# An attention and adapter block on one core: P V as eight 64x32 tiles, score bursts of two pairs on six banks

## What is computed

```python
h = _layernorm(x) * (1 + ca) + sa
qkv = (h @ qkv_w.T).reshape(B, S, 3, 16, 16)          # 16 heads of width 16
scores = jnp.einsum('bhqd,bhkd->bhqk', q, k) * scale
probs = jax.nn.softmax(scores, axis=-1)
out = jnp.einsum('bhqk,bhkd->bhqd', probs, v)
x = x + ga * (out @ proj_w.T + proj_b)
h = _layernorm(x) * (1 + cb) + sb
# 8 encoders and decoders are tried on h, the one with the least loss is chosen, and its
# adapter (W_down, W_up) is added to h @ W_base + b_base
x = x + gb * ffn(h)
```

## Time and profile before

| | before |
|---|---|
| median of 3 runs | 971.86 us |
| the profiled execution's own time | 975.65 us |
| its span in the trace | 973.8 us |
| busy: PE matmul | 938.1 us, 96% |
| busy: PE weight load | 489.1 us, 50% |
| busy: VectorE | 792.8 us, 81% |
| busy: ScalarE | 656.7 us, 67% |
| busy: GpSimd | 373.6 us, 38% |
| chain that ended last | PE 76%, DVE 10%, ACT 4%, DMA 3% |

### The profile page before, as it was taken

How to read it: one execution, slowest core, us unless ns; L and a number is a source line. 1 busy time by engine, 2 the same in 40 slices (tenths; PEclk the granted TensorE clock), 3 DMA queues, 4 the chain that set the end, 5 groups by cost and what they waited for, 6 DMA issues and landing times.

```text
span 973.8 us, 16714 instructions
## 1 busy us (share of the span) xinstructions
PE 938.1 (96%) x5890; PEld 489.1 (50%) x5890; DVE 792.8 (81%) x1629; ACT 656.7 (67%) x1295; POOL 373.6 (38%) x497
## 2 busy tenths in 40 slices
PE   6899999999999999999999999999999899999997
PEld 4443344434444555555444555645445465644486
DVE  4799989999788888877897888876887778888365
ACT  2148888888588677666679677575777756667930
POOL 4050265225366354121746645121655312115320
PEclk9889999999899999999999999999999999999999
DMA  7832061253444210555150511526123500141101
GB/s 179 142 73 45 23 115 58 60 122 82 70 75 77 59 45 25 83 82 168 48 86 20 94 57 35 83 54 170 52 64 53 77 8 29 41 129 59 30 6 50
DMA packets 51427, 68.78 MB, mean 71 GB/s; under 512 B 12347, under 2 KB 35648, under 8 KB 51332
## 3 DMA queue, kind: packets, MB, share of 16 engines
q1 hardware_dynamic: 50108, 66.84, 32.1%
q0 software_dynamic: 384, 0.79, 0.6%
q10 hardware_dynamic: 852, 0.09, 0.1%
HBM read 29.31 MB, written 12.59 MB: 43 GB/s over the span
## 4 chain that ended last, share of the span: by engine, by line
PE 76%; DVE 10%; ACT 4%; DMA 3%; SPq 2%; issue 2%; POOL 1%; ACTq 0%; DVEq 0%
PE pE L849 26%; PE pM L849 21%; PE pO L849 20%; PE pX L849 7%; DVE mx L1344 6%; DMA QO<-lo 2%; ACT P L1170 2%; SPq L1949 1%; DMA xin<-in_x 1%; DVE junk L1538 1%; ACT h2l_full L1257 1%; SPq L2009 1%; DMA P<-in_wmod 0%; DVE junk L1481 0%; ACT h1l_full L1211 0%
## 5 line engine op out<-in xcount | busy, mean ns | idle before, releaser
L1344 DVE TENSOR_REDUCE mx<-pM 128x1 f32<-128x512 f32 x458 | 298.6, 682 | 43.7 <-PE pM L849 41.6
L1170 ACT ACTIVATE P<-pM 128x512 f32<-128x512 f32 x464 | 260.2, 602 | 70.7 <-PE pM L849 69.4
L1344 DVE TENSOR_REDUCE mx<-pE 128x1 f32<-128x512 f32 x428 | 284.2, 681 | 28.9 <-PE pE L849 27.8
L1170 ACT ACTIVATE P<-pE 128x512 f32<-128x512 f32 x413 | 240.5, 602 | 83.4 <-PE pE L849 82.7
L849 PE MATMUL pO<-P,V 128*17 128x512 f32 x2048 | 261.0, 604 | 0.3 <-ACT P L1170 0.2
L849 PE MATMUL pM<-KO,QO 48*128 48x512 f32 x458 | 182.7, 456 | 8.2 <-DMA QO<-lo 6.5
L849 PE MATMUL pE<-KO,QO 48*128 48x512 f32 x428 | 179.0, 445 | 2.1 <-DVE mx L1344 1.3
L849 PE MATMUL pM<-QO,KO 50*128 50x512 f32 x464 | 174.1, 435 | 0.9 <-DVE mx L1344 0.5
L849 PE MATMUL pE<-QO,KO 50*128 50x512 f32 x413 | 170.7, 440 | 1.5 <-DVE mx L1344 1.0
L849 PEld LDWEIGHTS pM<-QO,KO 50*128 50x128 f32 x464 | 80.6, 188 | 85.0 <-issue 58.3
L849 PEld LDWEIGHTS pE<-QO,KO 50*128 50x128 f32 x413 | 73.8, 187 | 98.0 <-issue 76.5
(11 more groups left out here) (351 smaller groups left out, 1395.8 us busy)
## 6 DMA issues: line engine op xcount, KB each, us to landing
outs<-osb SPq DMA_DIRECT2D x31, 256.0 KB, 2.1
KO<-hi SPq DMA_DIRECT2D x56, 128.0 KB, 4.0
QO<-hi SPq DMA_DIRECT2D x56, 128.0 KB, 5.8
x<-in_x SPq DMA_DIRECT2D x20, 256.0 KB, 3.4
out<-x SPq DMA_DIRECT2D x16, 256.0 KB, 2.1
AT<-outs SPq DMA_DIRECT2D x15, 256.0 KB
asum<-wsum SPq DMA_DIRECT2D x15, 256.0 KB
KO<-lo SPq DMA_DIRECT2D x28, 128.0 KB, 4.1
```

The source lines that it names most:

```text
L1170: e.activation(P[:, u % 3, j, :], bank(s), ACT.Exp).then_inc(*empties(s))
L1344: e.tensor_reduce(mx[:, hq % 2, k:k + 1, kh], bank(s), AX.X, ALU.max, negate=True).then_inc(*empties(s))
```

## The change

- `BURST` goes from 3 to 2 pairs.
- A `PV` of the first 248 units (`ROWED`) becomes eight matmuls of 64 rows and 32 columns: four with keys 0 to 63 into `pO`, four with keys 64 to 127 into `pX`. The last eight units keep the old form.
- `pX` is therefore no longer lent while this runs, and scores and long steps share six banks.
- At the end of each group of eight units ScalarE copies `pX` as well, into `asum`, once the last division that reads `asum` is done; GpSimd adds `asum` to `osb`, and `oput` waits for that sum.
- A PV stands at each border of a unit, between two bursts, and long and short steps stand in the middle of a unit. So one unit is: two pairs, a long step (if one is ready), two pairs, a PV. `FULL = 99` keeps long steps away from the border.
- Some due times move by a unit; `mturn` comes later after the maxima.
- In the tail, three pieces of `half` are finished before the other three begin, the split of `wdn` into `wdh` and `wdl` on VectorE stands ahead of its last `base` sum, and `mid` waits for `wdh` alone before it starts.

```diff
-BURST = 3
+BURST = 2
-SHARE = (1.3, 1.8, 2.2, 2.4)
+SHARE = (0.8, 0.8, 0.8, 1.1)
...
+CAP = 2
+FULL = 99
+STEPS = 1
+MOVES = 2
+STILL = 1
+TURNS = 1
+ASIDE = 0
+BEHIND = 2
+ROWED = NU - 8
...
-        u = 200 if gi == 4 * NB - 1 else 16 * gi - 33
+        u = 200 if gi == 4 * NB - 1 else 16 * gi - 34
...
-                    u += (2, 2, 1, 0)[q]
+                    u += (3, 2, 1, 0)[q]
...
-        return [(("mmax", b), 1.2)]
+        return [(("mmax", b), 2)]
...
+        credit += SHARE[min(int(u) // UB, LAST)]
+        if at % 4 == 0:
+            while pv < at // 4 - BEHIND:
+                weigh(pv, u)
+                pv += 1
+            if credit < FULL and not (ASIDE and waiting["short"] and waiting["short"][0][0] == "mturn"):
+                continue
+        credit, filled = long(u, min(credit, CAP), STEPS)
+        for _ in range(TURNS):
             s = next_of("short", u)
...
                 taken = {self.turn[x][0] for x in unfinished}
-                bank = min((x for x in range(7) if x not in taken), key=lambda x: at.get(x, -1))
+                bank = min((x for x in range(6) if x not in taken), key=lambda x: at.get(x, -1))
...
-                    for j in range(4):
-                        a = mm(pO[32 * j:32 * j + HD + 1, :], V[:, b % 2, kb, 4 * (gi % 4) + j, :],
-                               P[:, u % 3, j, :], start=kb == 0, stop=kb == 7)
-                    a.then_inc(s_pv, 1)
+                    if u < ROWED:
+                        for r, o, done in ((0, pO, s_pv), (64, pX, s_pw)):
+                            for j in range(4):
+                                a = mm(o[32 * j:32 * j + HD + 1, :], V[r:r + 64, b % 2, kb, 4 * (gi % 4) + j, :],
+                                       P[r:r + 64, u % 3, j, :], start=kb == 0, stop=kb == 7)
+                            a.then_inc(done, 1)
...
-                    e.activation(osb[:, :], pO[:, :], ACT.Copy).then_inc(s_osb, 1)
+                    a = e.activation(osb[:, :], pO[:, :], ACT.Copy)
+                    if s[1] < ROWED:
+                        act.wait_ge(s_pw, s[1] + 1)
+                        act.wait_ge(s_at, S.normed[hq])
+                        a = e.activation(asum[:, :], pX[:, :], ACT.Copy)
+                    a.then_inc(s_osb, 1)
...
+                if kind == "oput":
+                    pool.wait_ge(s_osb, s[1] + 1)
+                    e.tensor_tensor(osb[:, :], osb[:, :], asum[:, :], ALU.add).then_inc(s_oadd, 1)
```

More of the change, by code:

```diff
@@ L366, in weigh @@
     def weigh(w, u):
+        if w % 8 == 7 and w < ROWED:
+            for s in [s for s in waiting["quiet"] if s[0] == "onorm" and ("osum", *s[1:]) in done]:
+                waiting["quiet"].remove(s)
+                put(s, u)
         out.append(("PV", w))
@@ L399, in order @@
                    for s in waiting["quiet"])
-        for _ in range(6 if moving and moving[0][1] == 4 * NB - 1 else 3):
+        for _ in range(4 if moving and moving[0][1] == 4 * NB - 1 else MOVES):
             if moving and (not held or u > 8 * SEQ.index((moving[0][1], 0)) - LEAD // 4 - 6) and (moving[0][1] < 3 or at >= 32 * (SEQ.index((moving[0][1] - 3, 1)) + 1)):
@@ L405, in order, with still @@
                     done["moved", out[-1][1]] = u
[L406 to L410, removed]
+        def still(n):
+            for _ in range(n):
+                s = next_of("quiet", u)
+                if s:
+                    put(s, u)
+        still(1)
         light = u < LIGHT or ready(u) < (1 if u >= UB * LAST else 2)
[L413 to L417, removed]
+        credit += SHARE[min(int(u) // UB, LAST)]
+        if at % 4 == 0:
+            while pv < at // 4 - BEHIND:
                 weigh(pv, u)
                 pv += 1
[L420 to L430, removed]
+            if credit < FULL and not (ASIDE and waiting["short"] and waiting["short"][0][0] == "mturn"):
+                continue
+        credit, filled = long(u, min(credit, CAP), STEPS)
+        for _ in range(TURNS):
             s = next_of("short", u)
@@ L473, in order @@
     fill(base[0], 1)
[L474 to L477, removed]
+    for p in range(3):
+        fill(first[1][p], 0)
+    now(("gsq", q, 0, 1), ("gsq", q, 1, 1))
+    for p in range(3):
+        fill(first[1][p], 1)
+    now(first[1][3], ("pick", q))
     fill(base[1], 0)
@@ L506, in __init__ @@
             self.nth[s] = kinds[s[0]]
+            if s[0] == "PV" and s[1] % 8 == 7:
+                self.normed[s[1] // 8] = kinds["onorm"]
+            if s[0] == "osum":
+                self.added[s] = kinds["oput"]
+            if s == ("E", 0, 0):
+                self.lent = uses[6]
+                assert all(self.turn[x][0] < 6 for x in unfinished)
             begun = begun or s[0] == "M"
             if s[0] == "E" and kinds["M"] == NM:
-                bank = min(range(5), key=lambda x: at.get(x, -1))
+                bank = min(range(4 if kinds["PV"] <= ROWED else 5), key=lambda x: at.get(x, -1))
             elif s[0] == "E":
                 taken = {self.turn[x][0] for x in unfinished}
-                bank = min((x for x in range(7) if x not in taken), key=lambda x: at.get(x, -1))
+                bank = min((x for x in range(6) if x not in taken), key=lambda x: at.get(x, -1))
                 burst = n
@@ L516, in __init__ @@
                 taken = {self.turn[x][0] for x in unfinished}
-                bank = s[1] % 5 if s[1] < LEAD else min((x for x in range(7) if x not in taken), key=lambda x: at.get(x, -1))
+                bank = s[1] % 5 if s[1] < LEAD else min((x for x in range(6) if x not in taken), key=lambda x: at.get(x, -1))
                 burst = n
@@ L523, in __init__ @@
                 if begun and not late:
-                    free = (5, 6) if not kinds["E"] or kinds["M"] == NM else range(7)
+                    free = (5, 6) if not kinds["E"] or kinds["PV"] > ROWED else (4, 5) if kinds["M"] == NM else range(6)
                 bank = min((i for i in free if i not in taken), key=lambda x: at.get(x, -1))
@@ L895, in tensor @@
                         pe.wait_ge(s_osb, u // 8)
-                    for j in range(4):
-                        a = mm(pO[32 * j:32 * j + HD + 1, :], V[:, b % 2, kb, 4 * (gi % 4) + j, :],
-                               P[:, u % 3, j, :], start=kb == 0, stop=kb == 7)
-                    a.then_inc(s_pv, 1)
+                    if u == 0:
+                        pe.wait_ge(s_free[6], S.lent)
+                    if u < ROWED:
[4 more added lines that the diff above has]
+                            a.then_inc(done, 1)
+                    else:
+                        for j in range(4):
+                            a = mm(pO[32 * j:32 * j + HD + 1, :], V[:, b % 2, kb, 4 * (gi % 4) + j, :],
+                                   P[:, u % 3, j, :], start=kb == 0, stop=kb == 7)
+                        a.then_inc(s_pv, 1)
                 elif kind == "mturn":
@@ L1098, in tensor @@
                     sl = slice(512 * h, 512 * h + 512)
-                    a = thrice(mm, o[0:H, :], wdh[:, c, :], wdl[:, c, :], h2h[:, c, sl], h2l[:, c, sl], c == 0, c == 1)
+                    mm(o[0:H, :], wdh[:, c, :], h2h[:, c, sl], c == 0, False)
+                    mm(o[0:H, :], wdh[:, c, :], h2l[:, c, sl], False, False)
+                    if b == LAST:
+                        pe.wait_ge(s_wdL, 2)
+                    a = mm(o[0:H, :], wdl[:, c, :], h2h[:, c, sl], False, c == 1)
                     if c == 1:
@@ L1615, in vector @@
                         a.then_inc(s_hL, 1)
-                elif s == ("mid", LAST, 0) and not piece:
+                elif s == ("base", LAST, 3) and not piece:
                     dve.wait_ge(d_wdn, 16 * NB)
-                    e.tensor_copy(wdh[:, :, :], wdn[:, :, :]).then_inc(*link.up())
-                    dve.wait_ge(*link.now())
+                    e.tensor_copy(wdh[:, :, :], wdn[:, :, :]).then_inc(s_wdL, 1)
+                    dve.wait_ge(s_wdL, 1)
                     e.tensor_tensor(wdl[:, :, :], wdn[:, :, :], wdh[:, :, :].bitcast(F), ALU.subtract).then_inc(s_wdL, 1)
```

19 lines of the change are left out of this document (12 added, 7 removed).

## The result

The change makes the kernel slower: 1030.03 us median (1024.42 to 1034.54, 4 runs) against 971.25 us, a ratio of 1.0596 with a 95% interval of 1.0566 to 1.0625. The forecast of 942 us had the wrong sign, and the measured time lies above the whole range, and above the main rival's own (970 to 1010) as well.

A forecast was written before the change was run, and what follows sets the result against it. TensorE was taken as the bound by a small distance. The terms +37.5 + 7 - 82 + 8 - 0.5 gave -30 us, so 971.9 - 30 = 942 us, own range 922 to 960, over all cases 920 to 994.

The forecast's parts named there:

- main rival: At the border between pairs and PV: it costs what it did, nothing saved; 988 us (970 to 1010), chance 0.38.
- What bounds the kernel: Whole kernel: TensorE is the bound by a small distance, its matmuls covering 96% of the span, VectorE 81%, ScalarE 67%.
- 57 us of waits: TensorE's weight loads: waits for maxima and exps in the four largest rows, 19.5 + 16.8 + 13.0 + 7.7 us.
- Part 1: TensorE's changes of kind: more runs of pairs (+23.6), PV (+7.5) and all else (+6.4), sum +37.5 us.
- Part 2: PV as eight tiles instead of four, both row halves running at once: 0.03 us more each, 248 times, +7 us.
- Part 3: Border between pairs and PV: with all tiles 64 rows high, the whole 0.33 us round trip is saved, -82 us.
- lower end: Border between pairs and PV: all of the round trip saved, 248 x 0.33 = -82 us; the upper end saves nothing.
- mid's row: Trace row where mid, 64 columns wide, follows a 128-column product after 0.23 us; taken as evidence for a free border.
- Part 4: ScalarE's second copy (+18.7 us) and GpSimd's sum (+40 us) at group ends: off the path, cost 0, up to +20.
- Part 5: Six banks and evener bursts: up to 49 us new VectorE waits replace the 57; +8 us (0 to +20) remains.
- 28 us of waits: In the 988 us case: VectorE catches up while TensorE is slower, so 25 to 30 us of waits come back.
- Part 6: Tail: mid waits for wdh alone, which ends earlier than wdl; between 0 and -0.7, taken as -0.5 us.

## Why the prediction was wrong, step by step

*What bounds the kernel:* right. TensorE's time from start to start explains the whole difference. But the 57 us of waits were misread: they are idle time of the weight loads, in which matmuls run. From start to start the waits of the pairs were 74 us before, the slower clock's share among them.

*Part 1, more runs, +37.5 us:* right. It is the largest single cause: +30 us by the traces, with the evener waits already taken off and some 5 us of clock in it.

*Part 2, eight tiles, +7 us:* right. The median PV run goes from 0.98 to 1.01 us, 0.03 x 248 = 7.4 us.

*Part 3, the border, -82 us:* **wrong, and the step on which the sign hung.** The value is 0: the round trip of 0.33 us is paid as before (the PV starts 0.34 us behind the last pair and takes 1.00). With 0 in place of -82 the forecast's own sum is +52, or 1024 us, near the 1030 measured. I took the lower end for mid's row, a narrow tile next to a wide one with no pause, and overlooked that mid is in the one-pass format while PV is float32. In float32 the same tile pays 0.14 us. The PV's own rows, 32 against 128 columns at equal height, were in the same format and nearer, and they had said "nothing saved". The Trainium skill's rule (TensorEngine Tiling (Array Packing), Key Properties), that a change of the tiling mode drains, held at this border; I had let the row of another format outweigh it. Mid's one-pass row still doesn't follow it.

*Part 4, the second copy:* I had 0, up to 20. Engine time is as worked out on GpSimd (+38 us); ScalarE has +25.6 where I had +18.7. The cost is 6 us by the ratios and 10 by the medians, not told apart from 0.

*Part 5, banks and evenness, waits equal and +8 us:* the waits of the pairs grew by 7 us, so the sum came out near, partly by luck: the order took 10 off, the bank, to which I had given a part of 8, put 14 on, and the tiles 3. The 53 runs of four pairs wait 98.7 - 53 x 1.14 = 38 us, within my 49, but the size was bounded by the wrong thing. I priced four pairs in a row by VectorE's rate and not by the round trip of a bank, about 1.26 us from a pair to the pair that reuses its banks. For the same reason the main rival was too low: it let 28 us of waits come back where the waits grew by 7, and so gave 988 us. With 44 + 7 in place of 44 - 28 it would have said 1023.

*Part 6, the tail, -0.5 us:* not told from 0.

What stays open: how the 12 us of the eight tiles divide beyond the 7.4 of the PV, how much of the four-pair runs' wait would go with both engines faster, and why the one-pass product of 64 columns pays nothing at its border.

## What to carry to other kernels

Ask of a row that is to price a border whether it has the same format as well as the same shape; a "free" neighbour in another format says nothing. Count the changes of kind that a schedule makes, since each costs 0.13 to 0.20 us here and a count of the order gives it before a run. And size a burst by the banks: a burst that uses all of them, or more pairs than there are pairs of banks, waits for a whole round trip through the engines that empty them. Read what a wait costs from start to start: the idle time of weight loads holds time in which matmuls run, and one stall can stand in two rows, the loads' and the matmuls'.

## What the runs showed that I had not expected

One PSUM bank was worth 97 us (972 to 1069) to a schedule of three-pair bursts that needed six, and 14 us to one of two-pair bursts that needed four. The new order, with its shorter burst, made the lost bank bearable, but it costs 32 us itself; the shorter burst in the old planner costs 91. And a third of VectorE's work (803 to 547 us busy) was worth only 17 us, although VectorE was busy 78% of the time.
